# Leaving out the 208 unread matmuls of a recurrent layer's kernel

## What is computed

```python
x = x + attn_layer(layernorm(x))      # recurrence over the 512 steps
x = x + expert_layer(layernorm(x))    # router, one of 4 experts, projection, layernorm

# the recurrence, for every step:
sa    = einsum('bhij,bhj->bhi', state, a_t)
state = state * d_t + sa[..., None] * b_t + v_t[..., None] * k_t
out   = einsum('bhij,bhj->bhi', state, r_t)

# the expert layer, for every token:
expert_idx = argmax(x @ W_router)
h = gelu(x @ W1[expert_idx] + b1[expert_idx])
y = layernorm(h @ Wo + bo + x)
```

## Time and profile before

| | us |
|---|---|
| median of three runs | 1195.27 (1194.85 to 1198.77) |
| the profiled execution | 1195.53 |
| its span, first to last instruction | 1193.7 |

### The profile page before, as it was taken

How to read it: one execution, slowest core, us unless ns; L and a number is a source line. 1 busy time by engine, 2 the same in 40 slices (tenths; PEclk the granted TensorE clock), 3 DMA queues, 4 the chain that set the end, 5 groups by cost and what they waited for, 6 DMA issues and landing times.

```text
span 1193.7 us, 19599 instructions
## 1 busy us (share of the span) xinstructions
PE 1054.8 (88%) x6099; PEld 713.3 (60%) x6099; DVE 940.2 (79%) x2283; ACT 605.3 (51%) x965; POOL 650.4 (54%) x885
## 2 busy tenths in 40 slices
PE   4676689999998999999998989999999999988976
PEld 2243356666565757666665757566666656666755
DVE  4468778898989888898988888898889888876320
ACT  2424364736465574637464564647364654733341
POOL 0246665665656656566656666665556566555200
PEclk9769899999999999999999999999999999999989
DMA  3324123342424233432424232333425233221110
GB/s 126 67 40 75 33 45 71 63 89 42 100 47 86 56 61 69 78 72 52 94 42 96 56 74 56 67 71 62 90 41 102 45 84 57 52 58 36 37 27 18
DMA packets 136496, 75.58 MB, mean 63 GB/s; under 512 B 15292, under 2 KB 129980, under 8 KB 136264
## 3 DMA queue, kind: packets, MB, share of 16 engines
q1 hardware_dynamic: 136392, 74.33, 31.0%
HBM read 11.35 MB, written 4.19 MB: 13 GB/s over the span
## 4 chain that ended last, share of the span: by engine, by line
PE 36%; DVE 20%; SPq 19%; issue 10%; ACT 8%; DMA 6%; POOL 0%; DVEq 0%; ACTq 0%; POOLq 0%
SPq L314 10%; SPq L301 6%; PE fin_b L564 6%; PE fin_a L564 5%; DMA val_rep<-val_c 5%; PE sa_ps L405 5%; DVE state L898 4%; PE mid_ps L356 4%; PE pre_a L356 3%; DVE upd L894 3%; PE var_ps L586 3%; ACT L600 3%; SPq L298 3%; DVE kv L871 2%; DVE s_a L884 1%
## 5 line engine op out<-in xcount | busy, mean ns | idle before, releaser
L1071 POOL TENSOR_TENSOR plus_kv<-state,kv 128x128 f32<-128x128 f32 x512 | 283.3, 553 | 406.1 <-DVE state L898 383.1
L405 PE MATMUL sa_ps<-s_a,con 128*128 128x128 f32 x1024 | 226.0, 303 | 55.8 <-DVE s_a L884 53.2
L405 PEld LDWEIGHTS sa_ps<-s_a,con 128*128 128x128 f32 x1024 | 172.3, 193 | 168.7 <-DVE s_a L884 137.7
L1063 POOL TENSOR_TENSOR s_r<-state,r_t 128x256 f32<-128x256 f32 x256 | 244.7, 956 | 3.3 <-DVE state L898 3.3
L894 DVE TENSOR_TENSOR upd<-sa_ps,b_t 128x128 f32<-128x128 f32 x512 | 146.2, 286 | 84.6 <-PE sa_ps L405 80.7
L898 DVE TENSOR_TENSOR state<-upd,plus_kv 128x128 f32<-128x128 f32 x512 | 191.8, 375 | 17.6
L884 DVE TENSOR_TENSOR s_a<-state,a_t 128x128 f32<-128x128 f32 x512 | 149.4, 292 | 18.5
L564 PE MATMUL fin_b<-h_e,mat 128*128 128x256 f32 x512 | 136.9, 394 | 4.0 <-ACT pick L770 4.0
L871 DVE TENSOR_TENSOR kv<-val_rep,k_t 128x512 f32<-128x512 f32 x128 | 117.8, 921 | 23.9 <-DMA val_rep<-val_c 23.3
L600 ACT ACT_TABLE_LOAD x101 | 129.6, 1283 | 1.8
L564 PE MATMUL fin_a<-h_e,mat 128*128 128x256 f32 x512 | 127.9, 379 | 0.0
(11 more groups left out here) (198 smaller groups left out, 1725.9 us busy)
## 6 DMA issues: line engine op xcount, KB each, us to landing
val_rep<-val_c SPq DMA_DIRECT2D x512, 64.0 KB, 2.4
rs_p<-row_rs SPq DMA_DIRECT2D x128, 64.0 KB, 2.1
x_in<-xT SPq DMA_DIRECT2D x16, 256.0 KB, 3.0
rs_p<-row_rk SPq DMA_DIRECT2D x64, 64.0 KB, 2.4
x_res<-xT SPq DMA_DIRECT2D x16, 256.0 KB, 3.0
rs_m<-row_frs SPq DMA_DIRECT2D x64, 64.0 KB, 2.1
rs_f<-row_ers SPq DMA_DIRECT2D x64, 64.0 KB, 2.1
rs_f<-row_lrs SPq DMA_DIRECT2D x64, 64.0 KB, 2.1
```

The costliest lines, as they stand in the source:

```text
L405: mm(sa_ps[:, 0:STATE], k("sum8"), s_a[:], start=True, stop=True).then_inc(s["sa"], 1)
L1063: tt(part, states, r.unsqueeze(2).broadcast_to([128, 2, N, B]), ALU.mult).then_inc(s["s_r"], 1)
L1071: tt(plus_kv[:, (t % 2) * STATE:(t % 2 + 1) * STATE], st(t), kv[:, at:at + STATE], ALU.add).then_inc(s["plus_kv"], 1)
```

## The change

All `keep` matmuls are left out, with their waits and with the count `fj_made`, which only they used. The entry "keep" goes from each of the three tables; the other entries are the same, only broken into lines differently. So each engine's order of all other instructions is the same.

```diff
-    "keep": (-7, 1, 1, 1, 14, 28, 62, 93, 94, 95, 95),          # AT
-    "keep": (-24, -23, -16, -8, -2, -1, 2, 6, 15, 15, 23, 26, 33, 36, 39, 51, 60, 62, 95, 95),   # AT_FIRST
-    "keep": (-18, -10, -7, -2, 1, 13, 19, 27, 28, 31, 32, 59, 59, 60, 86, 89, 91, 93),           # AT_LAST
...
-
-            fj_made = [0]
...
                     sums(var_ps, 0, "mean32", sq_m, "fj")
-                    fj_made[0] += 1
...
-                for n in range(len(c.place["keep"])):
-                    if at == c.place["keep"][n]:
-                        if fj_made[0]:
-                            pe.wait_ge(s["fln"], fj_made[0])
-                        mm(var_ps[:, 2 * C:4 * C], k("sum8"), con[:, 0:2 * C], start=True, stop=True, skip_group_check=True)
```

More of the change, by code:

```diff
@@ L31 @@
     "mix_r": -15, "mix_v": -15, "w2": -14, "th_d": -13, "rk": -13, "mix_g": -13, "kks": -13, "val_c": -12,
[L32 to L35, removed]
[2 rows of a table removed]
+    "v": -11, "cum": -10, "p": -10, "k2": -9, "val": -9, "r": -8, "kk": -8, "val_sb": -8, "k_t": -7,
+    "r_t": -7, "rec": -6, "a_t": -5, "rkb": -5, "g1": -4, "rkb_ps": -3, "kki": -3, "th_g": -3, "b_t": -2,
+    "g2": -2, "bonus": 0, "gate": 2, "bonus_b": 3, "x_res": 17, "gsq": 34, "grs": 35, "gj": 36, "fsq": 37,
[2 rows of a table added]
     "f2": (56, 56, 57, 57, 58, 58, 58, 58), "d_ers": 57, "y1": 59, "ec": 59, "ej": 59, "esq": 60, "ers": 60,
@@ L45 @@
 AT_FIRST = {
[4 rows of a table removed]
[L50 to L53, removed]
[3 rows of a table removed]
-    "pick_sb": 61, "h": 63, "router": 63, "y1b": 63, "best": 64, "onehot": 64, "masks": 64,
-    "h_e": (65, 65, 67, 68), "pick": 65,
[3 rows of a table added]
+    "w2": -14, "mix_g": -13, "kks": -13, "d_rk": -11, "v": -11, "val": -11, "k2": -11, "val_c": -10,
+    "cum": -10, "r": -10, "val_sb": -9, "rep": (-9, 4, 5, 11), "kk": -8, "r_t": -8, "a_t": -8, "p": -7,
+    "k_t": -7, "rkb": -6, "g1": -6, "rec": -6, "rkb_ps": -5, "kki": -5, "b_t": -4, "th_g": -3, "g2": -2,
+    "gate": -2, "bonus": -1, "bonus_b": 1, "x_res": 28, "gsq": 34, "grs": 35, "gj": 36, "gxh": 38, "fsq": 39,
+    "gaff": 39, "gg": 39, "wo": 40, "x2": 41, "fc": 41, "frs": 42, "d_frs": 42, "fj": 44, "x2x": 47, "xf": 47,
+    "fxh": 48, "hid": (51, 52, 57, 59), "kf": 52, "f1": (52, 52, 53, 54, 54, 55, 56, 56), "d_ers": 53,
+    "f2": (56, 57, 57, 58, 58, 58, 58, 58), "y1": 59, "ec": 59, "ej": 59, "esq": 60, "ers": 60, "pick_sb": 61,
+    "h": 63, "router": 63, "y1b": 63, "best": 64, "onehot": 64, "masks": 64, "h_e": (65, 65, 67, 68),
+    "pick": 65,
     "moe": (66, 66, 66, 67, 68, 69, 69, 69, 70, 70, 70, 70, 70, 71, 71, 71, 74, 75, 75, 75, 76, 76, 77, 77, 78, 79, 79, 80, 80, 80, 81, 81),
@@ L65 @@
     "xh0": -24, "d_rs1": -23, "c1": -22, "rs1": -21, "j1": -21, "d_rk": -20, "xn": -19, "th_w": -18,
[L66 to L71, removed]
[2 rows of a table removed]
[2 rows of a table added]
+    "cum": -11, "rep": (-11, 1, 3, 11), "k2": -9, "val": -9, "val_sb": -9, "r": -8, "kk": -8, "k_t": -7,
+    "r_t": -7, "rec": -6, "a_t": -5, "rkb": -5, "g1": -4, "rkb_ps": -4, "kki": -3, "g2": -3, "th_g": -2,
+    "b_t": -2, "gate": -2, "bonus": 0, "bonus_b": 13, "gsq": 34, "grs": 35, "gj": 36, "x_res": 38, "gxh": 39,
[2 rows of a table added]
     "f2": (56, 56, 57, 57, 58, 58, 58, 58), "d_ers": 58, "ec": 58, "y1": 59, "ej": 59, "router": 63, "h": 63,
```

## The result

The changed kernel takes 1212.87 us (median of four, 1208.13 to 1216.65) against 1195.06 us before: 1.0147 times as long, with a 95% interval from 1.0119 to 1.0174. The direction was right and the time lay in the range; of the forecast 27.4 us, 17.8 came.

The account below looks back on a forecast made before the run. Repeated scans were taken as bound by DVE's in-order queue, PE close behind. Preparation -0.4, chunks 0 and 1 +5.4, 14 scan starts +21.0, last scan and tail +1.4: +27.4 on 1195.5, forecast 1223 us, range 1200 to 1251.

Parts of the forecast that it names:

- The bound: Repeated scans: DVE's in-order queue binds, PE close behind; time freed on PE gives back at most 3.7 us a scan.
- The clock falls at the starts of the scans: Repeated scans: the clock falls about once in each, where router, `c0`, `masks` and `pick` are issued.
- The price of a fall: 14 scan starts, chunks 2 to 15: 1.8 us each, less 0.3 for earlier `pick`, +21.0 us in all.
- The credit for `pick`: Scan starts: `pick` could start 0.49 us earlier without the group ahead of it; credited at 0.3 us a start.
- Chunks 0 and 1: First two scans: about eight more low-clock stretches at 0.8 us, +6.4, less 1.0 for kept passes, +5.4 us.
- Last scan and tail: Bare steps, router, masks, `pick` and a 512-column pair at low clock, less 1.06 and 0.43 us: +1.4 us.
- (a): Scan starts: DVE hides most, leaving only the masks' 0.4 us at each of 14; 1202 us, chance 0.14.
- (b): Whole kernel: kept matmuls only cost, 8.8 us gained, 1187 us, chance 0.06; weak form, no effect, 1194 to 1196, 0.07.
- (c): Whole kernel: every us at low clock costs half a us, 64 us less 9; 1250 us, chance 0.12.

Follow-up runs that it names:

- e3_tiny: Kernel before with each of the 208 `keep` matmuls cut from 256 columns to 4, their places, waits and weight loads kept; 1212.7 us, ratio 1.0132.
- e4_behind_pick: Kernel before with the three `keep` matmuls of step 1 moved from ahead of `pick` to behind it; 1199.02 us, ratio 1.0022.
- the second profile: The changed kernel, same file, run and profiled again beside new runs of the kernel before; 1216.28 us, ratio 1.0171, span 1212.3 us.

## Why the prediction was right, and where its sum was not

**The bound.** Right in the repeated scans, and it is why little of the low time counted. They are bound by DVE, and its busy time didn't move (57.4 us in chunk 6 in both). PE lost 3 us of busy time there and nothing came back but 0.12 us for each start.

**The clock falls at the starts of the scans.** Right, and shown: e3_tiny has the queue and not the streaming, and loses as much as the whole change. But "about once in every repeated scan" was too much. In the two profiles 9 and 10 of the 14 starts had falls, and which ones changes from execution to execution.

**The price of a fall.** This is the term that was mis-sized, and the total lay in the range only because the range was wide. I took 1.8 us, less 0.3 for `pick`, and priced the start as if low clock could cover router, `c0`, masks and `pick` in one chain. A fall covers a part: in chunk 7 `c0` and the masks, with router and `pick` at full clock on both sides. And the +1.0 of `c0` isn't added to the masks' +0.4 in full. The masks start 1.83 us after `c0` in chunk 7 and 0.95 us after it in the earlier trace rows, where they follow `onehot`, so `c0` delays them by 0.88; and `h_e` had the 0.09 us of slack that I had read. DVE lost 1.14 us, where my terms for the two gave 1.4. The measured cost was 0.5 to 1.2 us. With nine or ten falls at about 0.9 us that is 8 to 9 us, against the 21.0 of the forecast; the term was more than twice too large.

**The credit for `pick`** was 0.3 us a start. It is 0.12 at best, and moving the group behind `pick` gained nothing (e4_behind_pick). DVE's queue doesn't wait there, as the prediction itself had said, so the credit should have been close to nought.

**Chunks 0 and 1.** +5.4 forecast, +2.9 and +5.6 in the two profiles. Low time rose by 23 us in the first profile (16.2 and 6.7) and by 34 in the second, 0.13 and 0.16 us for each. The agreement is in part luck, since chunk 0 alone took from 61.6 to 65.2 us in profiles in which its code was that of the kernel before. I also wrote that these chunks have 20 kept matmuls each; by their places, 12 fall in the scan of chunk 0 and 13 in that of chunk 1.

**Last scan and tail.** +2.9 forecast with its start, +3.4 measured. Chunk 14's router took 1.87 instead of 0.95 us, and bare scan matmuls 0.3 us more, as priced. The credit from the chain was partly real: step 28 of the last scan, in which six unread passes had stood ahead of the next scan matmul, went from 2.84 to 1.92 us.

**The rivals.** (a) was too small: DVE hides most of the low time, but it left 0.4 us for a start, where a fall cost 0.5 to 1.2. (b) falls in both forms, since the kernel is 1.3 to 1.7% slower and the clock falls at the starts. (c), half of all low time, falls clearly. Low time rose from 2 x 0.032 x 1193.7 = 76.4 to 2 x 0.067 x 1206.3 = 161.6 us; 85 us more cost 12.6 us, 0.15 for each. In the second profile it was 105 us more for 18.6, 0.18. The Trainium skill ("TensorE: Matmul & The Clock Gate", section "HAM oscillation — how this bites in real kernels") counts half of the throttled time as the price. This case's traces don't agree where another engine is the bound: 0.15 to 0.18 is about a third of that. Only the 16 expert passes in the tail, where the chain waits for PE alone, came near it (5.46 us with the clock low for 3.6 of them, 3.69 at full clock).

**What stays open.** Outside the ten steps around a start, a scan of the changed kernel takes 46.1 to 47.9 us from chunk 4 on (46.1 to 48.1 in the second profile), where before it took 46.5 to 46.8. The difference is at steps 16, 18 and 26, the last of them DVE's wait for the DMA that fills `val_rep`. On average it is 0.1 to 0.2 us a scan. It needs no falls: e4_behind_pick, with the clock at 1.00 in all these scans, has the same spread, 46.1 to 47.7 us, and is 0.2 us a scan above the kernel before. Whether the moments at which DMAs are issued set it, no run here tells.

## What to carry to other kernels

Matmuls that nobody reads can be worth their PE time if another engine is the bound and PE's load has light stretches ahead of something that this engine waits for. Price a fall of the clock by what waits in the stretch that it covers, not by the time it lasts: here 0.15 to 0.18 us for each us at low clock over the whole kernel and some 0.2 in chunk 0, against close to the full difference where PE's chain stands alone. So put them first into waits in which PE does nothing, as in the tail (3 us for 11 matmuls), and keep them from standing ahead of a matmul that is waited for.

## What the runs showed of the hardware that I had not expected

Where the clock falls isn't the same in each execution of the same program. It fell at 9 starts of a scan in one profile and at 10 in another, and only six chunks are in both lists. The times also spread more without the unread matmuls, 1208 to 1221 us over nine runs, against 1190 to 1200 over 67 runs of the kernel before; that the falls cause this spread is likely and not shown. Chunk 0 of the kernel before, which has light stretches even so, took between 61.6 and 65.2 us in profiles in which its code and its places were unchanged.

A matmul pass with 4 columns still takes 244 ns by its own duration, where one with 256 takes 400, with the same 128x128 weight load. 62.5 us of such busy time in e3_tiny left the clock where leaving the matmuls out did (0.938 and 0.933).
